# Storing rectified features a second time and letting the closing gathers add them in place

## The reference

```python
q, k, v = x @ Wq.T + bq, x @ Wk.T + bk, x @ Wv.T + bv
x1 = layernorm(x + softmax(q @ k.T / sqrt(512) + adj + adj) @ v)
feats = einsum('nf,hfd->hnd', x1, W)             # 8 heads of 64
dense = leaky_relu(e_self + e_neigh)             # from feats, a_self, a_neigh
dense = dense + (-1e10) * (1 - adj)
out1 = relu(softmax(dense) @ feats + b)
out = layernorm(x1 + out1)
```

## Time and profile before

| | |
|---|---|
| Median of 3 runs | 1740.49 us (1739.29 to 1741.75) |
| The profiled execution, time | 1742.69 us |
| The profiled execution, span | 1740.9 us |
| PE busy | 1630.1 us, 94% |
| DVE busy | 1104.7 us, 63% |
| POOL busy | 943.6 us, 54% |
| ACT busy | 630.9 us, 36% |
| 16 DMA engines, queue of SyncE / queue of GpSimd | 38.2% / 26.2% of the span |

### The profile page before, as it was taken

How to read it: one execution, slowest core, us unless ns; L and a number is a source line. 1 busy time by engine, 2 the same in 40 slices (tenths; PEclk the granted TensorE clock), 3 DMA queues, 4 the chain that set the end, 5 groups by cost and what they waited for, 6 DMA issues and landing times.

```text
span 1740.9 us, 22294 instructions
## 1 busy us (share of the span) xinstructions
PE 1630.1 (94%) x7748; PEld 748.6 (43%) x7748; DVE 1104.7 (63%) x1960; ACT 630.9 (36%) x1010; POOL 943.6 (54%) x891
## 2 busy tenths in 40 slices
PE   8989999999999999999999999999999999999820
PEld 3334443444444444444444444444444444444300
DVE  4343233667686768687857676777676776567455
ACT  5334322333343334333333333333333333345226
POOL 2000133667565756576657665765576566757351
PEclk9999999999999999999999999999999999999965
DMA  6443566676667666767667766766676767666157
GB/s 217 146 169 121 163 106 119 157 188 163 178 167 209 163 174 173 200 161 190 161 191 181 181 162 178 191 166 172 168 212 161 182 166 188 133 205 221 58 153 258
DMA packets 150482, 298.26 MB, mean 171 GB/s; under 512 B 16352, under 2 KB 16352, under 8 KB 147424
## 3 DMA queue, kind: packets, MB, share of 16 engines
q1 hardware_dynamic: 110944, 221.30, 38.2%
q0 software_dynamic: 39424, 75.52, 26.2%
HBM read 253.76 MB, written 42.99 MB: 170 GB/s over the span
## 4 chain that ended last, share of the span: by engine, by line
PE 84%; POOL 4%; issue 4%; DVE 3%; ACT 2%; DMA 2%; another core or an unknown queue 0%; SPq 0%; POOLq 0%; DVEq 0%; ACTq 0%
PE S L528 36%; PE O L588 35%; PE O L528 5%; PE X L528 4%; POOL sacc L489 2%; PE O L599 1%; DMA ring<-in_adjT 1%; POOL ring L466 1%; POOL ring L510 1%; DVE xT L891 1%; ACT ring L854 1%; ACT xT L736 1%; PE X L640 1%; DMA ring<-in_xT 1%; PE BC L623 0%
## 5 line engine op out<-in xcount | busy, mean ns | idle before, releaser
L528 PE MATMUL S<-yb,xT 128*128 128x512 f16 x3072 | 700.3, 379 | 0.0
L588 PE MATMUL O<-vring,ring 128*128 128x512 f16 x2928 | 672.6, 380 | 4.0 <-DVE ring L980 3.0
L528 PEld LDWEIGHTS S<-yb,xT 128*128 128x128 f16 x3072 | 301.0, 98 | 366.1 <-issue 6.0
L466 POOL DMA_DIRECT2D ring<-in_adjT x256 | 228.4, 892 | 404.0 <-ACT ring L736 361.7
L588 PEld LDWEIGHTS O<-vring,ring 128*128 128x128 f16 x2928 | 285.7, 98 | 341.7 <-issue 6.2
L481 POOL TENSOR_TENSOR ring<-pf,ring 128x512 f16<-128x512 f32 x224 | 282.5, 1261 | 242.8 <-ACT ring L736 238.0
L489 POOL TENSOR_TENSOR sacc<-sacc,pf 128x512 f32<-128x512 f32 x248 | 349.9, 1411 | 28.5 <-ACT ring L736 26.0
L736 ACT ACTIVATE ring<-S 128x512 f32<-128x512 f32 x256 | 152.4, 595 | 569.1 <-PE S L528 569.1
L952 DVE MAX8 cand<-piece 128x8 f32<-128x512 f32 x256 | 176.1, 688 | 221.5 <-DMA piece<-in_adj 220.8
L993 DVE TENSOR_TENSOR mx<-mx,ring 128x512 f32<-128x512 f32 x248 | 256.4, 1034 | 81.4 <-DMA ring<-in_adjT 81.4
L791 ACT ACTIVATE pf<-ring 128x512 f32<-128x512 f32 x256 | 160.7, 628 | 312.0 <-DVE ring L976 299.1
(11 more groups left out here) (115 smaller groups left out, 801.9 us busy)
## 6 DMA issues: line engine op xcount, KB each, us to landing
ring<-in_adjT POOLq DMA_DIRECT2D x256, 256.0 KB, 4.3
piece<-in_adj SPq DMA_DIRECT2D x256, 256.0 KB, 4.3
vring<-v_scratch SPq DMA_DIRECT2D x244, 256.0 KB, 3.8
ring<-in_xT SPq DMA_DIRECT2D x8, 1024.0 KB, 7.5
v_scratch<-vring SPq DMA_DIRECT2D x32, 256.0 KB, 2.3
y_scratch<-yb SPq DMA_DIRECT2D x8, 1024.0 KB, 4.9
yb<-y_scratch SPq DMA_DIRECT2D x8, 1024.0 KB, 7.1
xr<-in_x SPq DMA_DIRECT2D x32, 256.0 KB, 5.3
```

The costliest lines, as they stand in the source:

```text
L466: pool.dma_start(ring[:, c % SLOTS, :], adj_t[k * P:(k + 1) * P, b * QB:(b + 1) * QB], accum_op=ALU.add).then_inc(adj_in[c % 4], 16)
L528: mm = pe.matmul(psum, sta(a, k), mov(b, k), start=(k + a + b == 0), stop=(k == n - 1 and a == 1))
L588: mm = pe.matmul(O[j][:, :], ring16[:, e % SLOTS, a, j * P:(j + 1) * P], vring[:, e % NV, m, :], start=(k + a + m == 0), stop=(k == NT - 1 ...
```

## The change

Each tile of features is now stored twice. After the eviction into `fb`, DVE waits for it and writes `fr = max(fb, 0)`; SyncE stores `fr` in a new scratch tensor `positive_feats_scratch` and then `fb` in `feats_scratch` as before (the general path reads that one). Both stores count on the same semaphore. The gathers read the new tensor and have `compute_op=ALU.add`: they add the row to the tile of `x1r` in place. So the DVE pass L1152 is gone, `got` is gone, the passes of squares on ACT are gone, and all nine groups have their mean and variance from `bn_stats` and `bn_aggr`. Before the gathers of a group GpSimd waits for the reload of its `x1` tiles; for the last two groups, for the store of those tiles.

```diff
+            def store_feats(t):
+                sp.wait_ge(fr_set, t + 1)
+                sp.dma_start(fr_d[t * P:(t + 1) * P, :], fr[:, t % 2, :]).then_inc(f_out[t % 2], 16)
+                sp.wait_ge(f_set, t + 1)
+                sp.dma_start(f_d[t * P:(t + 1) * P, :], fb[:, t % 2, :]).then_inc(f_out[t % 2], 16)
...
             for k in range(2):
-                pool.wait_ge(f_out[k], NT // 2 * 16)
+                pool.wait_ge(f_out[k], NT * 16)
             pool.wait_ge(scan_set, 2 * NT)
-            pool.wait_ge(pv_done, PV_ALL)
             for e, tiles in enumerate(GROUPS):
+
+                if e < NB - 1:
+                    pool.wait_ge(x1r_in[e], 16)
+                else:
+                    for t in tiles:
+                        pool.wait_ge(x1_out[t % JB], NB * 16)
                 for t in tiles:
-                    pool.indirect_dma_start(out=got[:, t, :], out_offset=None, in_=f_d,
-                                            in_offset=bass.IndirectOffsetOnAxis(ap=pick[:, t:t + 1], axis=0)
-                                            ).then_inc(got_in[e], 16)
+                    pool.indirect_dma_start(out=x1r[:, t, :], out_offset=None, in_=fr_d,
+                                            in_offset=bass.IndirectOffsetOnAxis(ap=pick[:, t:t + 1], axis=0),
+                                            compute_op=ALU.add).then_inc(got_in[e], 16)
...
             def evict_feats(t):
                 dve.wait_ge(f_done, t + 1)
                 if t >= 2:
-                    dve.wait_ge(f_out[t % 2], t // 2 * 16)
+                    dve.wait_ge(f_out[t % 2], t // 2 * 32)
                 dve.scalar_tensor_tensor(out=fb[:, t % 2, :], in0=feats_bank(t), scalar=1.0 / (W_UP * X1_UP), in1=b1b[:, :],
                                          op0=ALU.mult, op1=ALU.add).then_inc(f_set, 1)
+                dve.wait_ge(f_set, t + 1)
+                dve.tensor_scalar(fr[:, t % 2, :], fb[:, t % 2, :], 0.0, None, ALU.max).then_inc(fr_set, 1)
...
             def last_norm():
                 for e, tiles in enumerate(GROUPS):
-                    first, last = tiles[0], tiles[-1] + 1
-                    if e < NB - 1:
-                        dve.wait_ge(x1r_in[e], 16)
                     dve.wait_ge(got_in[e], 16 * len(tiles))
                     for t in tiles:
-                        dve.scalar_tensor_tensor(out=got[:, t, :], in0=got[:, t, :], scalar=0.0, in1=x1r[:, t, :],
-                                                 op0=ALU.max, op1=ALU.add,
-                                                 accum_out=e_tot[:, t:t + 1]).then_inc(e_sum, 1)
-                    if e in BY_SQUARES:
-                        dve.wait_ge(e_sum, last)
-                        dve.tensor_scalar(e_mean[:, first:last, 0], e_tot[:, first:last], -1.0 / float(D) ** 1.5, None,
-                                          ALU.mult).then_inc(e_neg, 1)
-                        continue
-                    for k in range(len(TOGETHER)):
-                        if TOGETHER[k][-1] == e - 1:
+                        dve.bn_stats(e_st[:, t, :], x1r[:, t, :]).then_inc(stats_set, 1)
+                    for t in tiles:
+                        dve.wait_ge(stats_set, NT + t + 1)
+                        dve.bn_aggr(e_mean[:, t, :], e_st[:, t, :]).then_inc(mv_set, 1)
+                    for k in range(len(TOGETHER) - 1):
+                        if e == TOGETHER[k + 1][0]:
                             last_rstd(k)
-                    counted = sum(len(GROUPS[i]) for i in range(e) if i not in BY_SQUARES)
-                    for t in tiles:
-                        dve.wait_ge(e_sum, t + 1)
-                        dve.bn_stats(e_st[:, t, :], got[:, t, :]).then_inc(stats_set, 1)
-                    for n, t in enumerate(tiles):
-                        dve.wait_ge(stats_set, NT + counted + n + 1)
-                        dve.bn_aggr(e_mean[:, t, :], e_st[:, t, :]).then_inc(mv_set, 1)
```

More of the change, by code:

```diff
@@ L84, in adj_resnorm_kernel @@
         fb = sb("fb", [P, 2, D], F32)
+        fr = sb("fr", [P, 2, D], F32)
         bvb = sb("bvb", [P, D], F32)
@@ L162, in adj_resnorm_kernel @@
         f_d = dram("feats_scratch", [N, D], F32)
+        fr_d = dram("positive_feats_scratch", [N, D], F32)
         en_d = dram("e_neigh_scratch", [H, N], F32)
@@ L193, in adj_resnorm_kernel @@
         f_out = [sem("f_out0"), sem("f_out1")]
-        x1_hi, x1_lo, x1T_done, x1T_set, f_done, f_set = map(
-            sem, ("x1_hi", "x1_lo", "x1T_done", "x1T_set", "f_done", "f_set"))
+        x1_hi, x1_lo, x1T_done, x1T_set, f_done, f_set, fr_set = map(
+            sem, ("x1_hi", "x1_lo", "x1T_done", "x1T_set", "f_done", "f_set", "fr_set"))
         cand_set, cidx_set, top_set, gidx_set, pickf_set, scan_set = map(
@@ L204, in adj_resnorm_kernel @@
         GROUPS = [range(e * JB, (e + 1) * JB) for e in range(NB - 1)] + [range(NT - JB, NT - 2), range(NT - 2, NT)]
-        BY_SQUARES = (1, 3, 5)
         TOGETHER = ((0, 1), (2, 3), (4, 5), (6,), (7,), (8,))
@@ L208, in adj_resnorm_kernel @@
         got_in = [sem(f"got_in{e}") for e in range(NE)]
-        e_neg, e_square, e_sum, e_sd, e_chain, e_rstd, e_out, e_out_last, out_done = map(
-            sem, ("e_neg", "e_square", "e_sum", "e_sd", "e_chain", "e_rstd", "e_out", "e_out_last",
+        e_sd, e_chain, e_rstd, e_out, e_out_last, out_done = map(
+            sem, ("e_sd", "e_chain", "e_rstd", "e_out", "e_out_last",
                   "out_done"))
         x1r = xT[:, :, :, :].bitcast(F32).rearrange("p a c n -> p (a c n)").rearrange("p (t d) -> p t d", d=D)
-        got = ring[:, 0:NT, :]
         end = yb[:, 1].bitcast(F32).rearrange("p a c n -> p (a c n)")
@@ L221, in adj_resnorm_kernel @@
         e_nm = end[:, 576:576 + NT]
-        e_tot = end[:, 640:640 + NT]
         okw = end[:, 1024:1024 + 8 * NT]
@@ L372, in _ @@
                         t = b * JB + j
-                        sp.wait_ge(f_set, t + 1)
-                        sp.dma_start(f_d[t * P:(t + 1) * P, :], fb[:, t % 2, :]).then_inc(f_out[t % 2], 16)
+                        store_feats(t)
                         if j == JB - 1 and b + 3 < NB:
@@ L381, in _ @@
                     load_x1(e)
-            def store_feats(t):
-                sp.wait_ge(f_set, t + 1)
-                sp.dma_start(f_d[t * P:(t + 1) * P, :], fb[:, t % 2, :]).then_inc(f_out[t % 2], 16)
             def store_x1(t):
@@ L405, in _ @@
                 sp.dma_start(out[first * P:last * P, :].rearrange("(j p) n -> p j n", p=P),
-                             got[:, first:last, :]).then_inc(out_done, 16)
+                             x1r[:, first:last, :]).then_inc(out_done, 16)
             sp.wait_ge(out_done, 16 * NE)
@@ L410, in _ @@
             for k in range(2):
-                sp.wait_ge(f_out[k], NT // 2 * 16)
+                sp.wait_ge(f_out[k], NT * 16)
             def general():
@@ L843, in deviation @@
                 first, last = GROUPS[TOGETHER[k][0]][0], GROUPS[TOGETHER[k][-1]][-1] + 1
-                act.wait_ge(mv_set, NT + sum(len(GROUPS[e]) for e in range(TOGETHER[k][-1] + 1) if e not in BY_SQUARES))
-                act.wait_ge(e_square, sum(JB for e in BY_SQUARES if e <= TOGETHER[k][-1]))
+                act.wait_ge(mv_set, NT + last)
                 nc.scalar.activation(e_s[:, first:last], e_mean[:, first:last, 1], ACT.Sqrt, bias=eps[:, :],
@@ L853, in normalise @@
                         if t < NT - 1:
-                            nc.scalar.activation(got[:, t, :], got[:, t, :], ACT.Identity, bias=e_nm[:, t:t + 1],
+                            nc.scalar.activation(x1r[:, t, :], x1r[:, t, :], ACT.Identity, bias=e_nm[:, t:t + 1],
                                                  scale=e_r[:, t:t + 1]).then_inc(e_out, 1)
-            for k, groups in enumerate(TOGETHER):
-                for e in groups:
-                    if e in BY_SQUARES:
[L860 to L864, removed]
+            for k in range(len(TOGETHER)):
                 deviation(k)
@@ L1141, in last_rstd @@
                     dve.scalar_tensor_tensor(out=e_nm[:, t], in0=e_mean[:, t, 0],
-                                             scalar=float(D) ** 0.5 if e in BY_SQUARES else -1.0, in1=e_r[:, t],
+                                             scalar=-1.0, in1=e_r[:, t],
                                              op0=ALU.mult, op1=ALU.mult).then_inc(e_rstd, 1)
@@ L1146, in last_norm @@
                 for e, tiles in enumerate(GROUPS):
-                    first, last = tiles[0], tiles[-1] + 1
-                    if e < NB - 1:
-                        dve.wait_ge(x1r_in[e], 16)
                     dve.wait_ge(got_in[e], 16 * len(tiles))
                     for t in tiles:
-                        dve.scalar_tensor_tensor(out=got[:, t, :], in0=got[:, t, :], scalar=0.0, in1=x1r[:, t, :],
-                                                 op0=ALU.max, op1=ALU.add,
-                                                 accum_out=e_tot[:, t:t + 1]).then_inc(e_sum, 1)
```

(20 more changed lines are left out.)

## The result

The changed kernel takes 1754.32 us (median of 9 runs, 1749.34 to 1757.84) against 1741.75 us for the kernel before (9 runs). The ratio is 1.0067, with a 95% interval of 1.0052 to 1.0082: slower by 0.5 to 0.8%. The median forecast was 1752.0 us, the forecast span 1752.4 us, and the profiled execution has a span of 1752.2 us.

The account below looks back on a forecast made before the run. PE bounds the middle, the DMA engines the new end: first data at 1670.95, gathers 55.7, stores 22.7, tail 3.1 give a span of 1752.4, median 1752.0 us; 8-in-10 range 1731 to 1762, likeliest case 1744.5 to 1757.

Parts of the forecast that it names:

- The middle at 0: First 28 feature tiles: the extra DVE pass and store hide under PE, costing 0, at most 5 us.
- the last tile at 1.2 us: After the last feature eviction: added pass and second store delay the first gather 1.2 us, bounds 0.65 to 2.7.
- The sign named for a mistake: PE waits on DVE in the middle above 5 us in sum would show the term of 0 too small.
- The relief of DVE and ACT: At the end, 22 us of DVE passes and ACT's squares go, so neither engine holds up the end any longer.
- The DMA time of a gather with an add, 1.74 us: Closing gathers: each fills the DMA engines 1.74 us, taken from the direct adjacency add; bounds 0.94 and 2.3 us.
- GpSimd's time for one I leave at 1.28 us: Closing gathers: GpSimd's time for each gather with an add stays at the plain gather's 1.28 us.
- The gathers no longer keep GpSimd's pace: Closing gathers: DMA time of 1.74 us exceeds GpSimd's 1.28, so the engines set the pace instead.
- If the engines never idle: Closing stretch: condition for adding gathers, 55.7 us, and stores, 22.7 us, to a last byte at 1749.3 us.
- The landings that I expected to grow to over 15 us: Sign of being right: landings grow from gather to gather, well over 4 us at group 3, over 15 at the last.
- A free add: Rival for the closing gathers: the add costs no DMA time, 0.94 us a gather, span 8.5 us less; chance 0.21.
- The dearer add: Rival for the closing gathers: 1.97 or 2.3 us each, giving 1759 or 1770 us; chance 0.13, including an exposed middle.
- the level case: Rival: no change between the kernels, at 1.27 to 1.49 us of DMA time a gather; chance 0.08.

Follow-up runs that it names:

- The part alone: Kernel before plus only DVE's rectifying pass and each tile's second store, which the gathers wait for; end unchanged: ratio 1.0004 (0.9992 to 1.0016).
- the half rows: Changed kernel, but only the left 256 columns of the rectified features are stored and gathered with the add: ratio 1.0031 (1.0015 to 1.0047) to the kernel before.
- The plain gathers: Changed kernel with the add removed from the gathers, residual left out: 0.9975 of the kernel before, 1740.47 us; timed again in another set, 0.9981.
- the reorder: Kernel before with ACT's scaling of groups 2 and 3 moved ahead of group 5's squares: ratio 1.0004, timed again 0.9999.
- mixed gathers: Groups 0 to 4 gather plainly with DVE adding as in the kernel before, groups 5 to 8 gather with the add, ACT reordered: ratio 1.0038 (1.0019 to 1.0057).

## Why the prediction was right, and where a step of it failed

**The middle at 0, the last tile at 1.2 us.** Right. The part alone measured 0.7 us (-1.4 to 2.8), and the two profiles show 1.12 us more from the last eviction to the first gather. The sign named for a mistake, PE waits on DVE above 5 us in sum, was badly set: they were 7.2 us before (3.0, 2.7 and 1.5) and are 8.0 us now (3.5, 3.0 and 1.5).

**The relief of DVE and ACT.** Right in that giving ACT its work earlier gained nothing, though ACT is busy for the last 18 us before its end. Where gathers stay cheap, the relief is worth 5 us: 1.0004 with the added stores alone, 0.9975 with the relief as well.

**The DMA time of a gather with an add, 1.74 us.** Right as a size: 1.66 over all, 1.75 where it fills the engines. The direct adjacency add was a good stand-in, and the ceiling of 2.3 us was never near. The Trainium skill ("DMA: Bandwidth & Descriptors", section "SDMA does more than copy") puts the add unit inline with the data stream. It names no price; that the add would cost nothing is what the prediction drew from it, and that is not so for indirect adds either: 1.75 us against the plain gather's 0.94.

**"GpSimd's time for one I leave at 1.28 us."** This step failed. It is 1.86 us. Nothing in the trace before showed the instruction with an add; the direct add has one of 0.86 us, shorter than the plain gather's, which gave no warning. The step had to be bounded like the DMA time and was not. A hint stood in the rows: the adds went in 144 packets a tile against 80 for a gather, and I used it only for the engines. Per packet the gather's instruction is 0.946/80 = 11.8 ns, the adding one's 1.550/144 = 10.8 ns. That the time goes by packets is an inference; the half rows, which kept the 1.55 us, kept their packets as well, and fit it without proving it.

**"The gathers no longer keep GpSimd's pace."** Failed with it, by a little: they keep it, at 1.86 us, and the engines are 93.5% busy from the first byte to 1712. "If the engines never idle" was therefore off by only 6.5% of 39 us, 2.5 us. The first byte came 2.0 us later than I took (1672.95 for 1670.95), and the tail behind the last byte is some 1 us longer (4.1 for 3.1). The other way, a gather at 1.66 us instead of 1.74 gives 2.6 us back, the stores 0.4, and the overlap of the two queues (107.5% of 36 us) 2.7. These differences cancel, so the closeness of 1752.4 to 1752.2 is in part luck. The landings that I expected to grow to over 15 us stayed at 5 to 9, as the pace of 1.86 us is slower than the engines' 1.75.

**What decides.** Two limits lie close together, and the forecast knew one. GpSimd needs 1.86 us a gather and the engines up to 1.75. Slowing GpSimd's issue with cheap gathers is enough for 9.2 us of the 12; the engine time on top adds about 3 to 4.5. The engines were the forecast's whole case. At the old pace they might have cost as much as the sum says, but no run shows that.

**The rivals.** A free add would have given 1732. The plain gathers give a span of 1730.8 in one profile and 1741.7 in the other, 1740.5 and 1738.8 as medians. So the rival's arithmetic fits the one profile without the pauses below, but by the ratios (0.9975 and 0.9981 of 1740.5) it is 4 to 5 us too low, and its condition was false. The dearer add and the level case did not occur.

## What to carry to other kernels

Here a transfer with an add in it had two prices, one in the DMA engines (1.66 us for 0.94) and one on the engine that issues it (1.55 us for 0.95). Look for a row of each, and where there is none, bound both. Moving work off a busy engine pays only if what that engine waits for does not come later: here 22 us of DVE passes were removed and 18 us of GpSimd time put ahead of DVE. And when a sum is met by the total, check its terms in the new trace before believing it.

## What the runs showed that was not expected

**Pauses of DVE while the first results are stored.** In the kernel before, in one of two profiles of the plain gathers, in the kernel with the middle alone and in one of two with the reorder, DVE does single instructions 0.7 to 1.4 us apart for some 10 us from about 1700 on; two pauses are longer, 2.29 us in the reorder and 5.57 us in the middle alone. One execution of the plain gathers:

```profile
1703.64 0.17 DVE L1127 SCALAR_TENSOR_TENSOR yb<-yb 128x8 f32<-128x8 f32 x1
1704.79 0.17 DVE L1130 SCALAR_TENSOR_TENSOR yb<-yb 128x8 f32<-128x8 f32 x1 [0.98 <-DVE yb L1127]
1706.19 0.17 DVE L1133 SCALAR_TENSOR_TENSOR yb<-yb 128x8 f32<-128x8 f32 x1 [1.23 <-DVE yb L1130]
...
1712.49 0.18 DVE L1149 BATCH_NORM_AGGREGATE yb<-yb 128x2 f32<-128x6 f32 x1 [1.22 <-remote]
```

The other profile of the same kernel has none and a closing stretch of 67.8 us instead of 73.5; with the reorder it is 70.3 against 75.2. None of the eight profiles with slower or mixed gathers shows them. So some 5 us of the faster kernels come and go by execution, which is as much as the relief of DVE is worth. That the pauses make the whole difference is not shown, and their cause stays open.

**The instruction of an indirect transfer with an add** takes 1.55 us on GpSimd whether its rows are 2 KB or 1 KB, against 0.95 us without the add.
